# A sandwich of attention and feed-forward layers: another order of the matmuls within an attention step

## The reference

```
def _L0_attn_ref(x, Wqkv, bqkv, Wo, bo):
    kqv = x @ Wqkv + bqkv
    kqv = kqv.reshape(b, s, 3, NUM_HEADS, HEAD_SIZE)          # 16 heads of 32
    q, k, v = kqv[:, :, 0], kqv[:, :, 1], kqv[:, :, 2]
    scores = jnp.einsum('bsnh,btnh->bnst', k, q) / math.sqrt(HEAD_SIZE)
    scores = jnp.triu(scores) + -10000.0 * jnp.tril(ones, k=-1)
    attn = jax.nn.softmax(scores, axis=2)
    out = jnp.einsum('bnkq,bknh->bqnh', attn, v).reshape(b, s, 512)
    return out @ Wo + bo

x = x + _layernorm(_L0_attn_ref(_layernorm(x), ...))
x = x + _layernorm(_L0_ffn_ref(_layernorm(x), ...))   # silu(x Wg) * (x Wu), then Wd; int32 weights less 128, with scales
```

## Time and profile before

| what | us |
|---|---|
| three timed executions | 1710.94, 1705.3, 1711.95 |
| median | 1710.94 |
| profiled execution | 1705.27 |
| its span | 1703.5 |
| TensorE matmul busy | 1586.8 (93%) |
| VectorE busy | 959.2 (56%) |
| ScalarE busy | 740.5 (43%) |
| GpSimd busy | 598.3 (35%) |
| mean granted TensorE clock | 0.974 of full speed |

### The profile page before, as it was taken

One profiled execution on the slowest core, in us unless ns is written; L12 is line 12 of the kernel. 1 busy time (PEld: TensorE's weight loads), 2 busy tenths in 40 slices (PEclk: granted clock), 3 DMA queues, 4 the chain that ended last, 5 costly groups with the idle time before them and its releaser, 6 DMA issues.

```text
span 1703.5 us, 24930 instructions
## 1 busy us (share of the span) xinstructions
PE 1586.8 (93%) x9632; PEld 675.3 (40%) x9632; DVE 959.2 (56%) x1784; ACT 740.5 (43%) x1206; POOL 598.3 (35%) x808
## 2 busy tenths in 40 slices
PE   5889899999999999999998689999999999999997
PEld 2323333333433443334332234444444444444443
DVE  5766675678765767667777343463525252525344
ACT  5244555567555665655565343233222222222221
POOL 4243653666465656646665450020000000000000
PEclk8989999999999999999998899999999999999999
DMA  4311111123211332122224540122010111101000
GB/s 180 98 39 37 40 50 51 40 69 98 82 37 28 87 88 72 41 51 57 70 67 133 185 163 33 47 74 65 29 56 26 49 40 35 50 25 50 0 25 25
DMA packets 59398, 106.25 MB, mean 62 GB/s; under 512 B 11408, under 2 KB 11408, under 8 KB 59024
## 3 DMA queue, kind: packets, MB, share of 16 engines
q1 hardware_dynamic: 59280, 104.66, 19.8%
HBM read 54.02 MB, written 25.17 MB: 46 GB/s over the span
## 4 chain that ended last, share of the span: by engine, by line
PE 72%; DVE 12%; ACT 6%; POOL 6%; issue 4%; ACTq 0%; DVEq 0%; POOLq 0%
PE ps L854 25%; PE ps L775 16%; PE ps L871 12%; PE ps L838 10%; DVE mcol L1083 6%; PE ps L812 4%; ACT pt L953 4%; POOL pt L1289 3%; PE ps L788 2%; PE ps L796 2%; DVE st L980 1%; PE ps L742 1%; DVE v L1073 1%; POOL pt L1280 1%; POOL rs L1214 1%
## 5 line engine op out<-in xcount | busy, mean ns | idle before, releaser
L953 ACT ACTIVATE pt<-ps,nrm 128x512 f32<-128x512 f32 (+1 forms) x640 | 361.0, 645 | 378.2 <-PE ps L812 356.4
L854 PE MATMUL ps<-x2in,gu 128*128 128x512 f16 x2048 | 464.3, 380 | 0.0
L1083 DVE TENSOR_REDUCE mcol<-ps 128x1 f32<-128x512 f32 (+3 forms) x768 | 369.7, 547 | 88.9 <-PE ps L796 60.8
L854 PEld LDWEIGHTS ps<-x2in,gu 128*128 128x128 f16 x2048 | 200.7, 98 | 241.1 <-issue 2.6
L1211 POOL TENSOR_SCALAR rs<-mv 128x1 f32<-128x1 f32 x120 | 24.7, 205 | 665.3 <-DVE mv L984 659.7
L1158 DVE SCALAR_TENSOR_TENSOR hf<-ps,usc,sg 128x512 f32<-128x512 f32 x128 | 96.1, 751 | 265.2 <-PE ps L854 252.6
L1289 POOL TENSOR_TENSOR pt<-pt 128x1024 f32<-128x1024 f32 x96 | 226.9, 2381 | 12.4 <-ACT pt L953 11.7
L969 ACT ACTIVATE hh<-hf 128x512 f16<-128x512 f32 x128 | 80.7, 630 | 261.7 <-DVE hf L1158 248.1
L871 PE MATMUL ps<-wd,hh 128*128 128x512 f16 x512 | 194.0, 379 | 0.0
L871 PE MATMUL ps<-wd,hl 128*128 128x512 f16 x512 | 194.0, 379 | 0.0
L838 PE MATMUL ps<-pt,v 128*32 128x512 f32 (+3 forms) x1536 | 187.9, 516 | 1.5 <-DVE rec L1116 1.0
(11 more groups left out here) (116 smaller groups left out, 1622.3 us busy)
## 6 DMA issues: line engine op xcount, KB each, us to landing
qpack<-stage SPq DMA_DIRECT2D x192, 64.0 KB, 2.0
kpack<-stage SPq DMA_DIRECT2D x192, 64.0 KB, 2.0
xr<-in_x SPq DMA_DIRECT2D x32, 256.0 KB, 2.8
x1d<-xr SPq DMA_DIRECT2D x32, 256.0 KB, 2.4
x2d<-x2s SPq DMA_DIRECT2D x32, 256.0 KB, 2.0
x2in<-x2d SPq DMA_DIRECT2D x8, 1024.0 KB, 5.6
x1in<-x1d SPq DMA_DIRECT2D x8, 1024.0 KB, 5.8
out_x<-yy SPq DMA_DIRECT2D x32, 256.0 KB, 2.0
```

What stands on the lines that cost most here:

```text
L854: mm = pe.matmul(bk, GU[:, c, m, i * 128:(i + 1) * 128], x2in[:, 1 - k, :, p, c, :], start=p == 0 and c == 0, stop=p == 1 and c == 3)
L953: act.activation(Pt[:, PBUF[step], h, off:512], ps[:, BANK[job], off:512], ACT.Exp, scale=esc).then_inc(s_ex, 1)
L1083: mm = dve.tensor_reduce(mcol[:, n % 2, col:col + 1], ps[:, BANK["max", n, i, h], at:at + w], AX.X, ALU.max)
```

## The change

Three things change in the plan. Within a step the order is now: maxima, transposes and the other row jobs, the projection, the scores, and then ones and V products of the preceding step; before, it was maxima, ones and V products of the preceding step, scores, row jobs, projection. The evictions of a `qk` become a job of their own, `qk_out`, which stands behind the step's scores. And `projections(n)` moves some projections from step 2 (or 0, 2, 3) to others, chiefly step 4, with `row_work`'s room moved accordingly. With it the ring takes bank 5 in every step without a projection and gives bank 7 back at step 8.

```
@@ projections(n)
-        for i, s in enumerate(((0, 2, 3, 7) if b else (1, 3, 7, 9), (0, 1, 2, 3), (1, 3, 7, 9), (1, 3, 5, 8))[g]):
+        for i, s in enumerate(((0, 3, 4, 7) if b else (1, 3, 7, 9), (0, 1, 3, 4), (1, 3, 7, 9), (1, 3, 5, 8))[g]):
...
-        for i, s in enumerate(((), (7, 9), (0, 2, 5, 8), (0, 2))[g]):
+        for i, s in enumerate(((), (7, 9), (0, 4, 5, 8), (0, 4))[g]):
@@ row_work()
-            room[NS * n + s] = 18 - (24 if s in (0, 3) else 10 if s == NS - EARLY else 0)
+            room[NS * n + s] = 18 - (24 if s in (1, 4) else 10 if s == NS - EARLY else 0)
@@ order_of_jobs()
+def evicted(job):
+    return [job] + [("qk_out",) + job[1:]] * (job[0] == "qk")
...
-            if pend is not None:
-                summed = pend[1] == 1 and pend[2] < 4
-                if not summed:
-                    add(("den",) + pend)
-                add(("num",) + pend)
...
-            plan += [("score", n, j, kb, h) for h in range(4)]
...
+            summed = pend is not None and pend[1] == 1 and pend[2] < 4
+            if summed and pend[2] > 0:
+                plan += [("sum",) + pend + (0,), ("sum",) + pend + (2,)]
...
             plan += [job for job in here if job[0] in ("ln1_turn", "turn2")]
             plan += [job for job in here if job[0] not in ("ln1_turn", "turn2")]
...
-            if s in ends:
-                add(ends[s])
+            if s in within:
+                add(within[s])
+            plan += [("score", n, j, kb, h) for h in range(4)]
+            if s in within:
+                plan += evicted(within[s])[1:]
+            if pend is not None:
+                if not summed:
+                    add(("den",) + pend)
+                add(("num",) + pend)
+                if s == NS - 1:
+                    add(("den", n, 1, 0))
+                if last(*pend[1:]):
+                    plan += [("invert",) + pend[:2], ("normalise",) + pend[:2]]
@@ banks
     elif kind == "step":
+        FREE = [5]
         if 5 in RING:
             RING.remove(5)
-        if job[2] not in projections(job[1]) and FREE == [5]:
+        if 7 in RING and job[2] == 8:
+            RING.remove(7)
+        if job[2] not in projections(job[1]):
             RING.append(5)
...
     elif kind == "den":
-        if job[2:] == (1, 4):
-            RING.remove(7)
@@ scalar, gpsimd
-                elif kind == "qk":
+                elif kind == "qk_out":
```

More of the change, by code:

```diff
@@ L89, in projections @@
     if n + 2 < NG:
-        for i, s in enumerate(((0, 2, 3, 7) if b else (1, 3, 7, 9), (0, 1, 2, 3), (1, 3, 7, 9), (1, 3, 5, 8))[g]):
+        for i, s in enumerate(((0, 3, 4, 7) if b else (1, 3, 7, 9), (0, 1, 3, 4), (1, 3, 7, 9), (1, 3, 5, 8))[g]):
             out[s] = ("qk", n + 2, i % 2, i // 2)
     if n == 0:
-        for i, s in enumerate((0, 2, 5, 8)):
+        for i, s in enumerate((0, 4, 5, 8)):
             out[s] = ("vproj", 4 + i)
@@ L164, in order_of_jobs @@
     plan += [("ln1_turn", 6), ("norm_max", 1), ("ln1_turn", 7), ("inverses", 0), ("qk_scale", 0), ("split", 0)]
-    plan += [("inverses", 1), ("qk_scale", 1), ("split", 1), ("square", 2), ("qk", 0, 0, 0), ("qk", 0, 1, 0)]
-    plan += [("norms", 2), ("norm_max", 2), ("mjob", 0, 0), ("qk", 0, 0, 1), ("square", 3), ("mjob", 0, 1)]
-    plan += [("qk", 0, 1, 1), ("inverses", 2), ("split", 2), ("mjob", 0, 2), ("ones_rows", 0), ("packs", 0)]
+    plan += [("inverses", 1), ("qk_scale", 1), ("split", 1), ("square", 2)] + evicted(("qk", 0, 0, 0)) + evicted(("qk", 0, 1, 0))
+    plan += [("norms", 2), ("norm_max", 2), ("mjob", 0, 0)] + evicted(("qk", 0, 0, 1)) + [("square", 3), ("mjob", 0, 1)]
+    plan += evicted(("qk", 0, 1, 1)) + [("inverses", 2), ("split", 2), ("mjob", 0, 2), ("ones_rows", 0), ("packs", 0)]
     fill = [("qk", 1, i % 2, i // 2) for i in range(4)] + [("vproj", t) for t in range(4)]
     for i in range(3, len(LOTS)):
-        add(fill.pop(0))
+        plan += evicted(fill.pop(0))
         if i == 4:
@@ L190, in order_of_jobs @@
             add(("load_x2", 0))
-        ends = projections(n)
+        within = projections(n)
         for s, (j, kb) in enumerate(STEPS):
@@ L195, in order_of_jobs @@
             plan += [("dev", DEV_FOR[job[0]], job[1]) for job in here if job[0] in DEV_FOR]
+            if s == NS - EARLY and n + 1 < NG:
+                add(("mjoin", n + 1))
             lot, of = (s + EARLY, n + 1) if s < NS - EARLY else (s + EARLY - NS, n + 2)
@@ L198, in order_of_jobs @@
                 add(("mjob", of, lot))
-            if pend is not None:
-                summed = pend[1] == 1 and pend[2] < 4
-                if not summed:
-                    add(("den",) + pend)
-                add(("num",) + pend)
-                if summed and pend[2] > 0:
-                    add(("sum",) + pend + (0,))
-                    if s != 7:
-                        add(("sum",) + pend + (2,))
-                if s == NS - 1:
-                    add(("den", n, 1, 0))
-            plan += [("score", n, j, kb, h) for h in range(4)]
-            if s == 7:
-                add(("sum",) + pend + (2,))
-            if pend is not None and last(*pend[1:]):
-                plan += [("invert",) + pend[:2], ("normalise",) + pend[:2]]
+            summed = pend is not None and pend[1] == 1 and pend[2] < 4
+            if summed and pend[2] > 0:
+                plan += [("sum",) + pend + (0,), ("sum",) + pend + (2,)]
             if s == NS - EARLY and n + 1 < NG:
-                plan += [("mjoin", n + 1), ("mturn", n + 1)]
+                add(("mturn", n + 1))
             plan += [job for job in here if job[0] in ("ln1_turn", "turn2")]
@@ L339 @@
     elif kind == "den":
-        if job[2:] == (1, 4):
-            RING.remove(7)
         if job[2:] in ((0, 0), (1, 4)):
-            FREE = [5]
             take(job, 7)
@@ L927, in _ @@
                     stage = stages[n % 2]
-                    bk = ps[:, BANK[job], :]
+                    bk = ps[:, BANK[("qk",) + a], :]
                     e.wait_ge(s_small, SMALL["qk_scale", m])
```

## The result

The changed kernel takes 1762.8 us (median; 1761.4 to 1767.8) against 1708.3: a ratio of 1.032, 95% interval 1.029 to 1.036. The forecast was 1696, the range 1670 to 1725. The profiled execution has a span of 1760.8 us, 57.3 more than before.

What follows compares the result with a forecast made beforehand. TensorE was taken as the bound, with much of its time spent waiting. Groups 14 and 15 at -14, 0 and 1 at -6, and 2 to 13 at +10 sum to -10 us: forecast 1696, range 1670 to 1725.

Steps and rivals of the forecast that it cites:

- the row jobs' move ahead of S: Groups like 8: normalisation needing late GpSimd statistics now precedes step 7's exponentials (S: scores); GpSimd adds 3.2 us.
- Bank 5: Groups 2 to 13: projections wait for Q evictions now behind four exponentials; about 40 waits, 60 to 75 us.
- the waits merge: Rival, chance 0.18: other work catches up during bank-5 waits; groups 2 to 13 gain 20 us, total 1660 to 1675.
- And the 75 go: Groups 2 to 13: the old order's 75 us of TensorE losses were to disappear.
- the +10 that was written: Groups 2 to 13: 85 us of new waits against 75 lost before, so 10 us slower; bounds -25 and +35.
- Groups 0 and 1: First two attention groups: a small gain of 6 us, between 0 and 12.
- Groups 14 and 15: Last two attention groups: exponentials and select overlap other products; 14 us gained, bounds 4 and 22.
- The mis-sized term: Steps 14.8 to 15.3: weight fetch lands in 3.8 us, limiting steps to 3.7 us; 23 us for six, 11 gained.
- held by weights and GpSimd: Rival, chance 0.20: crowded fetches land later in the last groups, only 5 of 14 us come; total 1705, no change.
- The sign named for steps 15.0 to 15.3: Groups 15.0 to 15.3: none of TensorE's products would wait for GpSimd's select.
- the other signs: Groups 8 and 12 about 5 us longer, 10 shorter by 2 to 3, 14 and 15 about 97 us, clock above 0.9.
- The banks outweigh everything: Rival, chance 0.20: projections directly behind a Q step cost +35 us in groups 2 to 13; total 1731, or 1720.

Runs made afterwards that it cites:

- e2: The changed kernel with GpSimd's row statistics issued earlier, behind the preceding step's select; 1714.0 us, ratio 1.003 to the kernel before.
- e6: The changed kernel with row statistics behind the preceding step's select and the Q eviction directly behind its projection; 1697.9 us, ratio 0.994 to the kernel before.
- e14: The kernel before with only ScalarE's row normalisations moved ahead of the step's exponentials; 1768.1 us, ratio 1.035.
- e3: The changed kernel with the Q eviction directly behind its projection again; 1744.6 us, ratio 1.020 to the kernel before.
- e13: The changed kernel with the old tables (third projection in step 2, row-work room as before); 1738.7 us, ratio 1.018 to the kernel before.
- e10: The changed kernel with early row statistics, the Q eviction directly behind its projection, and the old tables; 1721.7 us, ratio 1.009 to the kernel before.
- e1: The changed kernel with ScalarE's row normalisations back behind the step's exponentials; 1722.7 us, ratio 1.008 to the kernel before.

## Why the prediction was wrong

Three terms of the sum for groups 2 to 13 failed, and all three are needed for the size of the miss. The one that made the kernel slower comes first.

*The step that failed* is the row jobs' move ahead of S. The mechanism was written down, for one place: "the row statistics of step 7 stand behind two of them, and a ScalarE normalisation that needs them now stands ahead of step 7's exponentials", priced at 3.2 us in three groups, 10 us in all. It is not a matter of step 7. It holds nearly wherever a step has a normalisation (59 of 64 wait), since GpSimd's statistics stand at the head of their step, behind everything of the step before. Moving the statistics up gives 44 us of the middle back (e2, e6), where 10 were priced, and the same move alone costs the old order 57 (e14). I had walked TensorE's queue instruction by instruction, and ScalarE's and GpSimd's only where a Q eviction led me. The Trainium skill, PSUM — Partial Sum Buffer, section Engine vs sequencer instructions, says that these queues are strict FIFO; the trace agrees: at 847.78 a normalisation had waited 4.35 us, with exponentials behind it whose scores had begun at 846.08. I used that sentence for evictions and not for normalisations.

*Bank 5: right in mechanism, wrong in price.* The waits came at their places. Two of group 8's four have nearly the size predicted (1.50 us from step 8.3 to 8.4, 1.7 predicted; 1.23 from 8.0 to 8.1, 1.4 predicted), the other two are about half (1.20 for 2.15, 0.98 for 1.75). In sum there is less: TensorE's projections wait 31 times and 36 us in the middle, 34 times and 40.1 us over the whole, where about 40 waits and 60 to 75 us were written; scores that take the same bank add 5.0 us in the middle. Their cost is 11 us by the middles of e3 and e6, 16 to 18 by the medians. Group 11, with one normalisation, shows how little a wait can be worth: it takes 53.9 us with 2.7 us of bank waits and 53.7 without any (e6). There the rival "the waits merge" was right. The Trainium skill's "Evacuate promptly", PSUM — Partial Sum Buffer, section Summary: rules for kernel authors, is borne out in sign, at that price.

*"And the 75 go": wrong, and the largest of the three.* The prediction's own sum without its bank waits (60 to 75) and its late statistics (10) is 681.5 - 75 + 85 - 70 to 85, so 607 to 622 us. e6, with no bank wait and early statistics, takes 690.8. The loss that was to go stayed nearly whole. Group 11 of e6 shows a part of it: M still stands behind exponentials in a step without a projection, and takes 1.36 and 1.48 us (751.43 to 752.79, 762.23 to 763.71) against 0.32 where nothing holds it (746.11 to 746.43):
```profile
746.11 0.39 PE L791 MATMUL ps<-stage 32*128 32x512 f16 x4
746.43 1.04 PE L778 MATMUL ps<-xTh,wh 128*128 128x512 f16 x4
...
751.43 0.84 PE L791 MATMUL ps<-stage 32*128 32x512 f16 x3
752.47 0.38 PE L791 MATMUL ps<-stage 32*128 32x512 f16 x1 [0.20 <-ACT pt L956]
752.79 1.04 PE L778 MATMUL ps<-wh,xTh 128*128 128x512 f16 x4
```
In the groups with row work the rest of the late statistics (66 us of waits) comes on top; how the whole divides is open. Against the +10 that was written, 69 to 84 us of gain did not come, the banks cost 49 to 64 less than priced, and the statistics 34 more: together the 55 that are missing. The first two errors nearly cancelled and hid one another. e2, with the bank waits and early statistics, takes 1714.0 us and would have lain inside the range, by luck.

*Groups 0 and 1: -6 predicted, -0.4 measured*, a sum of -8.8 in group 0 (70.9 to 62.1), which has no row work, and +8.3 in group 1 (59.7 to 68.0), which has it. With early statistics (e2) 121.4, -9.2.

*Groups 14 and 15: -14 predicted, -8.1 measured.* The first four steps gave 3.6 of the 4. Steps 14.8 to 15.3 gave 3.8 of 11: 30.3 us, not 23, at a DMA share of 0.68. The mis-sized term is the fetch. 3.8 us to landing was taken, so that one of the two converters would be served every 4.9 us, 3.7 us a step; the trace has a median of 4.5 and a longest of 8.1, and VectorE's conversions follow one another every 6.3 us (1003.22 to 1028.59), 4.8 us a step, 29 for the six. The rival "held by weights and GpSimd" had this, down to its warning that a late fetch reaches N: VectorE waits 6.03 us for a fetch, the inversion stands behind that conversion, and TensorE waits for the inversion:
```profile
1016.31 0.69 DVE L1152 TENSOR_SCALAR gu<-raw 128x1024 f16<-128x1024 int32 x1 [6.03 <-DMA raw<-in_wu]
1016.92 0.71 DVE L1111 STREAM_TRANSPOSE rec<-ps 128x512 f32<-128x512 f32 x1
...
1017.68 1.29 PE L842 MATMUL ps<-pt,ones 128*32 128x512 f32 x8 [3.23 <-DVE rec L1111]
```
The sign named for steps 15.0 to 15.3, no ones product waiting for the select, came nearly true: two waits and 1.5 us in the window of these steps, where before there were four and 8.8. Two waits of 3 us remain outside them, in steps 14.8 and 15.8. In the first, GpSimd's additions and then its own conversion stand ahead of the select:
```profile
997.49 4.65 POOL L1293 TENSOR_TENSOR pt<-pt 128x1024 f32<-128x1024 f32 x2
1002.12 1.04 POOL L1314 TENSOR_SCALAR gu<-raw 128x1024 f16<-128x1024 int32 x1
1003.12 1.42 POOL L1284 TENSOR_SCALAR_AFFINE_SELECT pt<-pt 128x256 f32<-128x256 f32 x2
...
1004.59 1.94 PE L842 MATMUL ps<-pt,ones 128*32 128x512 f32 x8 [3.00 <-POOL pt L1284]
```
Of the other signs, group 8 was to be 5 us longer and is 9.9, group 10 was to be 2 to 3 shorter and is 6.3 longer, and groups 14 and 15 were to take about 97 us at a clock above 0.9 and take 102.6 at 0.85.

*The rivals.* "The banks outweigh everything" had the right sign for the wrong reason, and 1731 as its end. Its own sentence "whatever delays an exponential now delays a projection too" was the warning: I did not list what could delay an exponential. The tables I took as a help; in the changed kernel they cost 24 us (e13).

Sum of the middle: 44 for late statistics, 11 for late evictions, 9 for the rest make the 65 measured. The 9 are themselves a difference: with the old tables the new order costs 25 even with both cures (e10, 706.3), and the tables give 15.5 of it back. What the 25 consist of is not settled, nor how the tables' cost with late statistics divides.

## What to carry to other kernels

When jobs are moved, list for each in-order engine what now stands ahead of its most urgent instruction, and ask of each when its own inputs arrive, back to the queue of the engine that makes them; normalisations that waited for nothing behind the exponentials cost 60 us ahead of them (e14). A short producer (1.2 us of statistics) belongs early in its engine's queue, before long jobs that wait for others. The length of a wait in a list is not its price: 36 us of bank waits were worth 11 to 18, and only removing them told so. And a loss that one counts on to go (here 75 us) needs an account of its own: ask what will hold the same instruction in the new order.

## What the runs showed of the hardware

The granted clock followed the waits. With the same instructions, groups 2 to 13 ran at 0.96 in the changed kernel and 0.99 before and in e1, e2 and e6. Groups 8 to 10 had 0.92 to 0.95, group 11, with a single late normalisation, 1.00. If every cycle not granted had been needed, that would be 746.4 x 0.04 - 681.5 x 0.01 = 23 us of the 65 (an estimate from the two mean clocks); it is an upper end, since a part of them fell on waiting. So the prices above are those of a wait and of the clock that goes with it; no run here parts the two. Small GpSimd instructions are dear for their size: three on one column per partition take 0.19, 0.55 and 0.27 us (846.54 on) and 1.24 us from the first start to the release of ScalarE, against 1.16 us for one of 512 columns.
